# Layer 2's self-attention in units of 256 queries instead of 128

## The reference

```
q, k, v: (B=4, H=16, S=256, dh=8)          # from x @ wqkv.T + bqkv
scores = einsum('bhqd,bhkd->bhqk', q, k) / sqrt(8)
attn = softmax(scores, axis=-1)
ctx = einsum('bhqk,bhkd->bhqd', attn, v)
```

## Time and profile before

| | us |
|---|---|
| median of three runs | 4377.2 |
| the three runs | 4367.52, 4377.2, 4378.14 |
| the profiled execution, its own time | 4368.58 |
| its span, first to last instruction | 4366.9 |
| mean granted clock of TensorE (1.00 is 2.4 GHz) | 0.868 |
| PE busy | 3340.7 (77%) |
| DVE busy | 2986.0 (68%) |
| ACT busy | 1871.6 (43%) |
| POOL busy | 352.6 (8%) |

### The profile page before, as it was taken

The page is one execution under the profiler, slowest core; times in us unless marked ns, Lnnn a source line. Parts: engine busy times, 40 slices in busy tenths (PEclk is TensorE's granted clock), DMA queues, the critical chain, the costliest instruction groups (busy, mean ns, idle before and its releaser), DMA issues. The chain is left out here.

```text
span 4366.9 us, 59636 instructions
## 1 busy us (share of the span) xinstructions
PE 3340.7 (77%) x24338; PEld 1728.6 (40%) x24338; DVE 2986.0 (68%) x4093; ACT 1871.6 (43%) x2165; POOL 352.6 (8%) x150
## 2 busy tenths in 40 slices
PE   6689999999999965577775886366654669577579
PEld 3433333333333323233333654222222346354357
DVE  4467777777777776498896545699998454546642
ACT  2255565556556542144443132444443235245233
POOL 0000000000000000000000000034442000000000
PEclk9799999999999978699998898565666799688789
DMA  2000000000000000000000200100000101010010
GB/s 81 16 13 11 8 8 15 8 8 15 8 8 13 3 7 18 14 14 9 9 1 15 106 2 21 27 0 0 0 0 0 40 2 39 9 39 1 1 38 8
DMA packets 22180, 69.30 MB, mean 16 GB/s; under 512 B 5393, under 2 KB 5905, under 8 KB 21010
## 3 DMA queue, kind: packets, MB, share of 16 engines
q1 hardware_dynamic: 21906, 65.47, 5.1%
HBM read 49.07 MB, written 0.52 MB: 11 GB/s over the span
## 5 line engine op out<-in xcount | busy, mean ns | idle before, releaser
L1050 PE MATMUL banks<-L0x_ring,L0x_context_rows 128*101 128x512 f32 x1600 | 734.7, 602 | 3.6 <-ACT L0x_ring L1096 3.6
L1106 ACT COPY L0x_ring<-banks 128x1024 f32<-128x1024 f32 (+1 forms) x416 | 387.1, 982 | 567.7 <-PE banks L1038 567.7
L1038 PE MATMUL banks<-L0x_q_thirds,L0x_context_thirds 32*128 32x512 f32 x4800 | 607.8, 617 | 28.4 <-ACT L0x_ring L1106 18.1
L1134 DVE TENSOR_TENSOR L0x_ring<-L0x_ring,L0x_greatest 128x2048 f32<-128x2048 f32 (+1 forms) x208 | 469.6, 2266 | 11.3 <-ACT L0x_ring L1106 9.7
L1150 DVE TENSOR_TENSOR L0x_maxima<-L0x_maxima,L0x_ring 128x1024 f32<-128x1024 f32 (+1 forms) x288 | 322.7, 1162 | 219.2 <-ACT L0x_ring L1106 219.2
L1050 PEld LDWEIGHTS banks<-L0x_ring,L0x_context_rows 128*101 128x101 f32 x1600 | 253.9, 167 | 455.9 <-issue 450.0
L1096 ACT ACTIVATE L0x_ring<-L0x_ring 128x2048 f32<-128x2048 f32 (+1 forms) x208 | 386.0, 1856 | 16.6 <-DVE L0x_ring L1134 16.2
L1038 PEld LDWEIGHTS banks<-L0x_q_thirds,L0x_context_thirds 32*128 32x128 f32 x4800 | 239.0, 188 | 376.8 <-issue 312.2
L1544 ACT ACTIVATE L1x_probs<-banks 128x2048 f32<-128x2048 f32 (+1 forms) x112 | 196.6, 1756 | 259.3 <-PE banks L1474 217.2
L1577 DVE TENSOR_REDUCE L1x_maxima<-banks 128x3 f32<-128x1203 f32 (+1 forms) x176 | 241.5, 1372 | 87.5 <-PE banks L1443 87.4
L1443 PE MATMUL banks<-L1x_k,L1x_q 32*128 32x401 f32 x1024 | 179.9, 586 | 120.6 <-DVE L1x_maxima L1577 105.1
(11 more groups left out here) (943 smaller groups left out, 5245.5 us busy)
## 6 DMA issues: line engine op xcount, KB each, us to landing
L0x_q_thirds<-L0x_q_context SPq DMA_DIRECT2D x192, 64.0 KB, 2.0
L1f_expert_weights<-in_L1f_experts SPq DMA_DIRECT2D x16, 512.0 KB, 9.6
L2f_expert_weights<-in_L2f_experts SPq DMA_DIRECT2D x8, 512.0 KB, 5.4
L3a_expert_weights<-in_L3a_experts SPq DMA_DIRECT2D x8, 512.0 KB, 5.8
L3f_expert_weights<-in_L3f_experts SPq DMA_DIRECT2D x8, 512.0 KB, 5.9
L1x_k<-L1x_k_rows SPq DMA_DIRECT2D x64, 50.0 KB
L0x_context_thirds<-in_context_thirds SPq DMA_DIRECT2D x1, 2496.0 KB, 14.2
L1x_context<-in_context SPq DMA_DIRECT2D x4, 600.4 KB, 5.3
```

The lines of the kernel that those rows point to most:

```text
L1038: mm = pe.matmul(k.ps[:, i, :], thirds[group_rows(i), slot, t, :], q_thirds[group_rows(i), u // 2 % 2, t, :], start=t == 0, stop=t == 2)
L1050: mm = pe.matmul(k.ps[0:CW, bank, :], rows1[0:height(j), j, :], ring[0:height(j), s % RING, i, :], start=s == FIRST[u] and i == 0, stop=s ...
L1106: act.copy(ring[0:r, s % RING, 2 * p:2 * p + len(pair), :], k.ps[0:r, 2 * p:2 * p + len(pair), :]).then_inc(copied, 1)
L1134: dve.tensor_tensor(o, o, greatest[:, u % 2, None, :].broadcast_to([P, len(js), 512]), ALU.subtract).then_inc(shifted, 1)
```

## The change

The unmasked call gets a function of its own, `attend_whole_batches`; `self_attention` keeps its text and now serves only the causal calls. A unit is now one batch and one group of four heads with all 256 queries: 16 units. The diff's core:

```
-            self_attention(k, "L2f", q, kk, v, y, H, d, causal=False)
+            attend_whole_batches(k, "L2f", q, kk, v, y, H, d)

+    units = [(b, g) for b in range(B) for g in range(groups)]
+        low = k.sb(ctx_name + "_minus_max", [P, 2, TPB, P], ctx=ctx)
+        qs = k.sb(ctx_name + "_q_shifted", [P, 2, S], ctx=ctx)
+        probs = k.sb(ctx_name + "_probs", [P, 4, TPB * S], ctx=ctx)
+                def scan(u):
+                    if u:
+                        pe.wait_ge(reduced, u)
+                    for it in range(TPB):
+                        for h in range(4):
+                            mm = pe.matmul(k.ps[:, h, whole(it)], queries(u)[row(h), tile(it)], keys(u)[row(h)], start=True, stop=True)
+                    mm.then_inc(scanned, 1)
+                def turn(u):
+                    pe.wait_ge(reduced, u + 1)
+                    if u:
+                        pe.wait_ge(exped, 2 * u - 1)
+                    for it in range(TPB):
+                        mm = pe.transpose(k.ps[:, 6, tile(it)], low[:, u % 2, it, :], k.ident[:])
+                    mm.then_inc(turned, 1)
+                def score(u):
+                    pe.wait_ge(shifted, u + 1)
+                    if u:
+                        pe.wait_ge(copied, u)
+                    for j in range(TPB):
+                        for h in range(4):
+                            mm = pe.matmul(k.ps[:, 4 + h, whole(j)], keys(u)[row(h), tile(j)], qs[row(h), u % 2, :], start=True, stop=True)
+                    mm.then_inc(scored, 1)
+                def values(u):
+                    b, g = units[u]
+                    pe.wait_ge(exped, 2 * u + 2)
+                    for j in range(TPB):
+                        for h in range(4):
+                            mm = pe.matmul(k.ps[row(h), 4, 0:S], v[:, b * TPB + j, 4 * g + h, :], probs[:, h, whole(j)],
+                                           start=j == 0, stop=j == TPB - 1)
+                    mm.then_inc(summed, 1)
+                scan(0)
+                turn(0)
+                scan(1)
+                for u in range(U):
+                    score(u)
+                    if u + 2 < U:
+                        scan(u + 2)
+                    if u + 1 < U:
+                        turn(u + 1)
+                    values(u)
...
+                for u, (b, g) in enumerate(units):
+                    act.wait_ge(scored, u + 1)
+                    act.activation(probs[:, 2:4], k.ps[:, 6:8, :], ACT.Exp).then_inc(exped, 1)
+                    act.activation(probs[:, 0:2], k.ps[:, 4:6, :], ACT.Exp).then_inc(exped, 1)
+                    act.wait_ge(summed, u + 1)
+                    act.copy(yT[:, b * TPB:(b + 1) * TPB, g, :], k.ps[:, 4, 0:S].rearrange("p (t j) -> p t j", t=TPB)).then_inc(copied, 1)
...
+                def reduce(u):
+                    dve.wait_ge(scanned, u + 1)
+                    if u >= 2:
+                        dve.wait_ge(turned, u - 1)
+                    dve.tensor_reduce(low[:, u % 2, :, 31::32], k.ps[:, 0:4, :].rearrange("p h (i n) -> p i h n", i=TPB), X, ALU.max,
+                                      negate=True).then_inc(reduced, 1)
+                def shift(u):
+                    dve.wait_ge(turned, u + 1)
+                    if u >= 2:
+                        dve.wait_ge(scored, u - 1)
+                    dve.tensor_tensor(qs[:, u % 2, :], queries(u), k.ps[:, 6, 0:S], ALU.add).then_inc(shifted, 1)
+                reduce(0)
+                for u in range(U):
+                    shift(u)
+                    if u + 1 < U:
+                        reduce(u + 1)
```

More of the change, by code:

```diff
@@ L554, in _, with attend_whole_batches, row, queries @@
                     o = k.ps[:, t, 0:BOTH].rearrange("p (h e) -> p h e", e=32)
+                    dve.reciprocal(rden[:, t, :], o[:, :, dv]).then_inc(recip, 1)
+                    dve.wait_ge(recip, t + 1)
+                    dve.tensor_tensor(y[:, t], o[:, :, 0:dv], rden[:, t, :, None].broadcast_to([P, heads, dv]), ALU.mult).then_inc(normed, 1)
+def attend_whole_batches(k, ctx_name, qT, kT, v, y, heads, dv):
+    groups = heads // 4
+    units = [(b, g) for b in range(B) for g in range(groups)]
+    U = len(units)
+    with ExitStack() as ctx:
+        low = k.sb(ctx_name + "_minus_max", [P, 2, TPB, P], ctx=ctx)
+        qs = k.sb(ctx_name + "_q_shifted", [P, 2, S], ctx=ctx)
+        probs = k.sb(ctx_name + "_probs", [P, 4, TPB * S], ctx=ctx)
+        yT = k.sb(ctx_name + "_y_columns", [P, TILES, groups, P], ctx=ctx)
+        rden = k.sb(ctx_name + "_reciprocal_sums", [P, TILES, heads], ctx=ctx)
+        with k.stage() as (block, signal):
+            scanned, reduced, turned, shifted, scored, exped, summed, copied, upright, recip, normed, cleared = (signal() for _ in range(12))
+            def row(h):
+                return slice(32 * h, 32 * h + 32)
+            def queries(u):
+                b, g = units[u]
+                return qT[:, g, b * S:(b + 1) * S]
+            def keys(u):
+                b, g = units[u]
+                return kT[:, g, b * S:(b + 1) * S]
+            def tile(j):
+                return slice(j * P, (j + 1) * P)
+            def whole(j):
+                return slice(j * S, (j + 1) * S)
+            @block.tensor
+            def _(pe):
+                def scan(u):
[21 more added lines that the diff above has]
+                def values(u):
+                    b, g = units[u]
+                    pe.wait_ge(exped, 2 * u + 2)
[14 more added lines that the diff above has]
+                    values(u)
+                pe.wait_ge(copied, U)
+                for t in range(TILES):
+                    for g in range(groups):
+                        mm = pe.transpose(k.ps[:, t, g * P:(g + 1) * P], yT[:, t, g, :], k.ident[:])
+                    mm.then_inc(upright, 1)
+            @block.scalar
+            def _(act):
+                for u, (b, g) in enumerate(units):
[4 more added lines that the diff above has]
+                    act.copy(yT[:, b * TPB:(b + 1) * TPB, g, :], k.ps[:, 4, 0:S].rearrange("p (t j) -> p t j", t=TPB)).then_inc(copied, 1)
+            @block.vector
+            def _(dve):
+                dve.memset(low[:], 0.0).then_inc(cleared, 1)
+                dve.wait_ge(cleared, 1)
+                def reduce(u):
[14 more added lines that the diff above has]
+                        reduce(u + 1)
+                for t in range(TILES):
+                    dve.wait_ge(upright, t + 1)
+                    o = k.ps[:, t, 0:groups * P].rearrange("p (h e) -> p h e", e=32)
```

## The result

The changed kernel takes 4354.1 us (median of five runs, 4350.07 to 4357.77) against 4377.2 (five runs, 4367.52 to 4378.46). The ratio of the two sets of runs (not that of the two medians, which is 0.9947) is 0.9952, 95% interval 0.9938 to 0.9967: faster by 14 to 27 us, and the whole interval lies beyond 0.3%. The profiled execution took 4354.1 us itself.

A forecast was written before the change was run, and what follows sets the result against it. No engine full: a chain of waits bounds the stage. 3482.7 + 6.7 + 14 x 4.83, then 3.54, ends at 3560.5 against 3577.51, 17.0 us less; 4377.2 - 17.0 = 4360, range 4347 to 4371.

The forecast's parts named there:

- The chain stays and each step falls short of doubling: Changed stage's unit: values to copy 1.12, copy to scores 0.51, scores to exponentials 1.20, exponentials to values 2.00; 4.83 us for 5.96.
- Columns of four heads: Scores and values on PE: doubling columns from 128 to 256 adds 0.42 and 0.41 us, less than double.
- rival 1: 256-long columns of four heads overlap worse on PE: scores and values cost double, period 5.4, total 4368; chance 0.08.
- 3.07 for four row tiles: Skill's speedup rule for scores and values on PE: 0.13 us more in each step, 3.9 in 15 periods, sum 4364.
- The values' 0.41: Values' products on PE: 16 instructions of 256 columns take 1.06 us, 0.41 more than 0.65 for 128 columns.
- Scan, reduction, turn and shift cost nothing: DVE and PE work beside the chain stays hidden under the 4.83 us period, so it was costed at nothing.
- the reduction has 1.0 us to spare: DVE's reduction ends 0.7 us into the next period; the scan could start as late as 1.7 without harm.
- the loop: DVE's own round of reduction 2.31, scan at most 1.13, turn 0.47, shift 0.42: 4.4 us, under the period of 4.83.
- Start and clock: Stage start at 1.2 GHz: scan from 3474.70, first exponentials at 3482.7; at 2.4 GHz it would be 3480.9.
- the period at half clock: One unit at 1.2 GHz taking 6.7 us after the first exponentials; bounds none and three such periods.
- The tail: After the last exponentials 3.54 us up to the turning back at 3560.5; what lies behind that stays the same.
- Rivals 2 and 3: Late DVE reduction makes values queue behind the scan, chance 0.05; clock at 1.2 GHz all stage, total 4391, chance 0.04.

The follow-up runs named there:

- The two runs that take the parts apart: Changed kernel with scan one unit ahead, before the scores: 4361.63 us; kernel before (128-query units) with scan two ahead: 4375.42 us.
- one_exp: Changed kernel with one exponential instruction over 2048 columns in place of two over 1024: 4363.27 us, ratio 0.9976.
- early: Changed kernel scoring heads 2 and 3 without waiting for the copy, heads 0 and 1 after it: 4345.93 us, ratio 0.9940.

## Why the prediction was right

The time (4360 forecast, 4354.1 measured), the direction and the mechanism hold: no engine is full, a chain of four steps sets the pace, and each step falls short of doubling. Point by point:

- *The chain stays and each step falls short of doubling.* Right. Three of its four steps came to within 0.01 us and the fourth to 0.02; the period is 4.85 for a forecast of 4.83. The two runs that take the parts apart show that it is the size of the units that pays, and `one_exp` that 5.3 us of it need the exponentials in two instructions.
- *Columns of four heads.* My price of 0.42 for 256 columns instead of 128 (rival 1 said double) is what the scores show: 1.15 long instead of 0.73. The prediction's estimate from the Trainium skill's 3.07 for four row tiles ("TensorE: Matmul & The Clock Gate", "Measured speedup vs the span model") would have made it 0.55; the trace doesn't agree with it for the columns added here. The values' 0.41 could not decide this, as the prediction has it, without the price of a product by itself. The trace of before has that price: in the linear products ahead of the stage (line 321, 128 rows, 512 columns, clock 1.00) 32 instructions take 13.97 us, 0.109 per 128 columns, and here a round of four heads adds 0.42 / 4 = 0.105 for 128 more.
- *Scan, reduction, turn and shift cost nothing.* Right in the steady periods, but "the reduction has 1.0 us to spare" was wrong: that counted until the scan would delay the values of its own unit, and left out that a later scan and shift also make the next reduction late. I had the loop as well, at 4.4 us with the scan's full length, and put the two bounds beside each other as if the first were the binding one. The loop is 4.23, the spare 0.62. Nothing hung on it here; it did set the limit of the version with early scores.
- *Start and clock.* The first exponentials came 7.59 after the first scan (8.0 forecast). The term that failed was the period at half clock, 6.7 of which I took one: the clock was back at 1.00 before the first exponentials, and the first period was 5.47. It lost 0.6 to the second reduction, which the late second scan (2.09 long) had put back; I had not counted that. First exponentials and first period together took 1.6 us less than forecast, and the stage gained 1.3 more than 17.0, within the bounds given. That the clock then held at 1.00 was a bet on the rows of other stretches, and it came true with PE busy 69% of the time, not the 76% of the forecast.
- *The tail.* "The tail behind is the same" was wrong in its time: the turning back took 5.15 us before and 3.72 after, and 2.3 us less lie behind its start, in both pairs of profiles. The same instructions ran at another clock.
- *The other 5 us of the median.* The difference of the medians, 23.1, is larger than the stage's 18.3. Of the 4.8 us between them, 2.3 are the tail's. The rest is, as far as the runs tell, their luck: the median of the kernel before, from which the forecast was taken down, was high at 4377.2, as the 18 and 19 runs beside the experiments have 4373.88 and 4374.28, and runs of either kernel scatter over 7 to 19 us. The interval of the ratio (14 to 27 us) holds both 18.3 and 20.6. How the clock falls in each of the unprofiled runs was not seen.
- *Rivals 2 and 3* (a late reduction, half clock all through) didn't come. The run with the reduction doubled shows what something near them costs: mean clock 0.70, the stage 38 us longer.

## What to carry to other kernels

When no engine is full and every unit passes through the same chain of short steps, write the chain down once at the present size and once at the doubled size, from rows of instructions with the larger shape. What each step falls short of doubling, times the number of units left, is the gain; work off the chain must then be tested as a loop of its own, round to its own next start, and not only against the next thing that waits for it. The next gain is in the wait that covers more than it must, here a copy of one bank that held up the scores of four.

## What the runs showed of the hardware that was not expected

- A filled gap moved a half-clock stretch rather than removing it from the changed kernel (start 1.00 throughout, then 0.50 over the last unit and the tail), while in the kernel before a like filling left the whole stage at 1.00. Each is one profiled execution.
- With one scan of 0.96 us moved in front of the scores, a loss of 0.22 us a unit in the chain, the one profiled execution had three stretches at 0.50 in the middle of a stage that otherwise held 1.00; each made one unit 1.6 us longer. With 1.14 us of reduction added a unit the mean clock of the stage was 0.82, with the reduction doubled 0.70. A small wait may thus cost more by the clock than by itself.
- Products of two heads at a time are not as dear as I had them: the two pairs of `early` took 1.69 us for 16 instructions, against 1.15 for four heads at once, where I had expected 1.73 of issue and 0.3 of drain. The second pair began while the first still ran: from 3522.55 on, the profile, which models the ends, has six of the instructions in flight where it had four before.
